# Two linear-attention layers with film conditioning: the film projection with the conditions stationary in four 32-column groups, its matrix moving, and the prologue in another order

## The reference, cut to what matters

```python
xn = layernorm(x)
q = softmax(xn @ Wq + bq, axis=features of a head)
k = softmax(xn @ Wk + bk + mask, axis=tokens)
v = (xn @ Wv + bv) * mask
y = q @ (k.T @ v)                         # per head, 8 heads in layer 0, 16 in layer 1
scale, shift = split(silu(emb) @ W_emb + b_emb)     # (8, 1024): the film projection
h = layernorm(y) * (1 + scale) + shift
x = x + silu(h) @ W_out + b_out
```

## Time and profile before

| | us |
|---|---|
| median of 3 runs (lowest to highest) | 915.04 (914.07 to 915.22) |
| the profiled execution | 913.57 |
| its span | 911.8 |
| PE busy | 865.9 |
| DVE busy | 717.8 |
| ACT busy | 536.2 |
| POOL busy | 382.9 |
| granted clock, mean over the span | 0.966 |

### The profile page before, as it was taken

How to read it: one execution, slowest core, us unless ns; L and a number is a source line. 1 busy time by engine, 2 the same in 40 slices (tenths; PEclk the granted TensorE clock), 3 DMA queues, 4 the chain that set the end, 5 groups by cost and what they waited for, 6 DMA issues and landing times.

```text
span 911.8 us, 14285 instructions
## 1 busy us (share of the span) xinstructions
PE 865.9 (95%) x5405; PEld 494.7 (54%) x5405; DVE 717.8 (79%) x1508; ACT 536.2 (59%) x911; POOL 382.9 (42%) x328
## 2 busy tenths in 40 slices
PE   4689999999999999899999999999999999999967
PEld 4248555475654655445455555555464555555544
DVE  5786987787867879989787878778697878777674
ACT  4256284854748647394765747383856647484713
POOL 1223253443434535453453544553443635455402
PEclk9697999989989999999999999999999999999988
DMA  9824124351643613434232534434442414323222
GB/s 324 334 47 93 59 47 105 90 142 59 185 105 76 156 58 93 104 93 105 48 91 66 111 79 93 105 93 105 71 108 50 108 59 100 98 47 93 47 47 93
DMA packets 168629, 90.86 MB, mean 100 GB/s; under 512 B 134736, under 2 KB 144240, under 8 KB 168560
## 3 DMA queue, kind: packets, MB, share of 16 engines
q1 hardware_dynamic: 168560, 89.94, 39.3%
HBM read 39.60 MB, written 16.78 MB: 62 GB/s over the span
## 4 chain that ended last, share of the span: by engine, by line
PE 73%; DVE 14%; issue 5%; ACT 4%; POOL 2%; DMA 1%; SPq 1%; DVEq 0%
PE ring L411 59%; PE ring L444 6%; PE att_ps L411 4%; PE film_ps L411 3%; DVE sb_w_lo L692 1%; DVE sb_y_stats L931 1%; DVE sb_kt_or_y L927 1%; POOL sb_ht_lo L1176 1%; DVE sb_v_or_q L887 1%; DVE sb_q_max L890 1%; ACT sb_tanh L1053 1%; ACT sb_k_or_qt L1031 1%; ACT sb_kq_hi L1039 1%; ACT sb_xh_or_h L1060 1%; DVE sb_v_or_q L859 1%
## 5 line engine op out<-in xcount | busy, mean ns | idle before, releaser
L411 PE MATMUL ring<-sb_w_hi,sb_xt_hi 128*128 128x512 f16 x512 | 194.8, 380 | 2.3 <-DVE sb_k_max L803 2.2
L411 PE MATMUL ring<-sb_w_lo,sb_xt_hi 128*128 128x512 f16 x512 | 194.8, 380 | 0.0
L411 PE MATMUL ring<-sb_w_hi,sb_xt_lo 128*128 128x512 f16 x512 | 194.6, 380 | 0.0
L1026 ACT ACTIVATE sb_kt_or_y<-sb_kt_or_y,sb_y_add,sb_y_rstd 128x512 f32<-128x512 f32 x64 | 46.9, 804 | 177.9 <-DVE sb_y_add L939 177.9
L1176 POOL TENSOR_TENSOR sb_ht_lo<-sb_xh_or_h,sb_ht_hi 128x512 f16<-128x512 f32 x60 | 68.5, 1174 | 114.5 <-ACT sb_ht_hi L1021 114.5
L411 PE MATMUL ring<-sb_xt_hi,sb_w_hi 128*128 128x512 f16 x256 | 98.1, 383 | 8.6 <-DVE sb_xt_lo L968 8.6
L411 PE MATMUL ring<-sb_xt_lo,sb_w_hi 128*128 128x512 f16 x256 | 98.0, 383 | 0.0
L411 PE MATMUL ring<-sb_xt_hi,sb_w_lo 128*128 128x512 f16 x256 | 98.0, 383 | 0.0
L411 PE MATMUL ring<-sb_w_hi,sb_ht_hi 128*128 128x512 f16 x240 | 92.0, 383 | 1.9 <-ACT sb_xh_or_h L1011 1.5
L411 PE MATMUL ring<-sb_w_lo,sb_ht_hi 128*128 128x512 f16 x240 | 91.8, 382 | 0.0
L411 PE MATMUL ring<-sb_w_hi,sb_ht_lo 128*128 128x512 f16 x240 | 91.3, 380 | 0.0
(11 more groups left out here) (174 smaller groups left out, 1832.2 us busy)
## 6 DMA issues: line engine op xcount, KB each, us to landing
out<-sb_x SPq DMA_DIRECT2D x15, 1024.0 KB, 5.1
sb_x<-out SPq DMA_DIRECT2D x8, 1024.0 KB, 6.1
sb_x<-in_x SPq DMA_DIRECT2D x7, 1024.0 KB, 8.2
sb_mask_raw<-in_mask SPq DMA_DIRECT2D x16, 256.0 KB, 5.8
sb_wemb<-in_L_cond_film_emb_W SPq DMA_DIRECT2D x8, 512.0 KB, 4.9
sb_w_stage<-in_L_cond_Wk SPq DMA_DIRECT2D x2, 1024.0 KB, 6.1
sb_w_hi<-in_L_cond_W_emb SPq DMA_DIRECT2D x1, 1536.0 KB, 15.9
sb_w_lo<-in_L_cond_W_emb SPq DMA_DIRECT2D x1, 1536.0 KB, 17.1
```

The source lines that it names most:

```text
L411: last = nc.tensor.matmul(out, lhs, rhs, start=(n == 0), stop=(n == len(pairs) - 1))
L1026: nc.scalar.activation(kt_or_y[:, t, :], kt_or_y[:, t, :], ACT.Identity, bias=y_add[:, t:t + 1], scale=y_rstd[:, t:t + 1]).then_inc(yh_rea ...
```

## The change

The conditions become the stationary operand, in `emb_wide`, eight blocks of 128x32 of which 24 columns are zero, and 128x512 pieces of `W_emb` the moving one. `film_product(layer, half)` makes 512 of the 1024 outputs with eight f32 matmuls: block k goes to the column group k % 4, so it writes the partitions 32 (k % 4) and up of `film_ps`, and each group sums two of the eight blocks. The result lies with conditions on partitions, in four parts. `copy_film` copies it to `film_rows`, and `turn_film` makes eight f32 matmuls with 128x128 of `film_rows` stationary and a 128x8 selection matrix `pick` moving, which adds the four parts and turns them into the layout that `gather_film` reads.

Layer 0's halves stand in the prologue and behind V tile 1 of step 0, `turn_film(0)` behind XT of step 0. Layer 1's halves stand in steps 6 and 7, `turn_film(1)` behind the first K tile of step 8, and `gather_film(1)`, `bound_film(1)` and `film_tables(1)` move from step 5 to step 8. The loads of layer 1's matrix go from eight of 512 KB in steps 0 to 4 to two pairs of 1024 KB in steps 5 and 7. In the prologue the mask is transposed first, x's transposes run tile by tile, DVE's list is in another order, and POOL's `x_power(1)` stands ahead of `add_bias(0, 0)`.

```diff
-        wemb = sb("wemb", [P, 2, KE, P], F32)
+        wemb = sb("wemb", [P, C, D], F32)
...
-        emb = sb("emb", [P, KE, B], F32)
-        emb_half = sb("emb_half", [P, KE, B], F32)
-        emb_tanh = sb("emb_tanh", [P, KE, B], F32)
+        emb_wide = sb("emb_wide", [P, KE, 32], F32)
+        pick = sb("pick", [P, B], F32)
+        film_rows = sb("film_rows", [P, 2, D], F32)
+
+
+        emb, emb_half, emb_tanh = (film_rows[:, 0, i * KE * B:(i + 1) * KE * B].rearrange("p (k b) -> p k b", k=KE)
+                                   for i in range(3))
...
-            def load_wemb0(begin, end):
-                for half in range(2):
-                    rows = wemb_d[0][half * E // 2:(half + 1) * E // 2, :].rearrange("(k p) n -> p k n", p=P)
-                    sp.dma_start(wemb0[half][:, :, begin:end], rows[:, :, begin:end]).then_inc(wemb0_loaded[begin > 0], 16)
-
-            def load_wemb1(n):
-
-                if n:
-                    sp.wait_ge(film_summed, 2 * C + 2 * n)
-                for j in (2 * n, 2 * n + 1):
-                    sp.dma_start(wemb[:, j % 2], wemb_d[1].rearrange("(k p) n -> p k n", p=P)[:, :, j * P:j * P + P]
-                                 ).then_inc(wemb_loaded[j % 2], 16)
+            def load_wemb0(half):
+                n = slice(half * D, half * D + D)
+                for part in range(2):
+                    rows = wemb_d[0][part * E // 2:(part + 1) * E // 2, :].rearrange("(k p) n -> p k n", p=P)
+                    sp.dma_start(wemb0[part][:, :, n], rows[:, :, n]).then_inc(wemb0_loaded[half], 16)
+
+            def load_wemb1(half):
+
+                sp.wait_ge(w_ready[1], O_ + 1)
+                if half:
+                    sp.wait_ge(film_half, 3)
+                for part, dst in enumerate((wemb, w_stage)):
+                    rows = wemb_d[1][part * E // 2:(part + 1) * E // 2, :].rearrange("(k p) n -> p k n", p=P)
+                    sp.dma_start(dst[:], rows[:, :, half * D:half * D + D]).then_inc(wemb_loaded, 16)
...
-                if 2 <= u <= 4:
-                    load_wemb1(u - 1)
+                if u in (B - 3, B - 1):
+                    load_wemb1(u > B - 3)
...
-            load_wemb0(0, 2 * P)
+            sp.dma_start(mask_rows, mask0_d.rearrange("b (t p) -> (b t) p", p=P)).then_inc(mask_rows_loaded, 16)
+            sp.dma_start(emb, emb_d).then_inc(emb_loaded, 16)
+            load_wemb0(0)
...
-            load_wemb0(2 * P, 2 * D)
+            load_wemb0(1)
...
-            load_wemb1(0)
...
-            def sum_film(layer, js):
-
-                if 0 in js and layer == 0:
+            def film_product(layer, half):
+
+                if layer == 0:
                     pe.wait_ge(emb_ready, 1)
-                for j in js:
-                    if layer == 0:
-                        pe.wait_ge(wemb0_loaded[j > 1], 32)
-                        w = lambda k: wemb0[k // 4][:, k % 4, j * P:j * P + P]
-                    else:
-                        pe.wait_ge(wemb_loaded[j % 2], 16 * (j // 2 + 1))
-                        w = lambda k: wemb[:, j % 2, k, :]
-                    product(film_ps[:, j * B:j * B + B], [(w(k), emb[:, k, :]) for k in range(KE)]).then_inc(film_summed, 1)
+                    pe.wait_ge(wemb0_loaded[half], 32)
+                    w = lambda k: wemb0[k // 4][:, k % 4, half * D:half * D + D]
+                else:
+                    pe.wait_ge(wemb_loaded, 32 * (half + 1))
+                    w = lambda k: (wemb, w_stage)[k // 4][:, k % 4, :]
+                if half:
+                    pe.wait_ge(film_copied, 2 * layer + 1)
+                for k in range(KE):
+                    g = slice(k % 4 * 32, k % 4 * 32 + 32)
+                    last = nc.tensor.matmul(film_ps[g, :], emb_wide[:, k, :], w(k), start=(k < 4), stop=(k >= 4))
+                last.then_inc(film_half, 1)
+
+            def turn_film(layer):
+
+                pe.wait_ge(pick_ready, 1)
+                pe.wait_ge(film_copied, 2 * layer + 2)
+                for j in range(2 * C):
+                    n = j % C * P
+                    last = nc.tensor.matmul(film_ps[:, j * B:j * B + B], film_rows[:, j // C, n:n + P], pick[:], start=True, stop=True)
+                last.then_inc(film_summed, 1)
...
-                    pe.wait_ge(w_scale_ready, 4 + u - 1)
-                    sum_film(1, (2 * u - 2, 2 * u - 1))
                     sum_w(1, u - 1)
-                if u == 5:
+                if u == B - 2:
+                    pe.wait_ge(w_scale_ready, 8)
+                if u in (B - 2, B - 1):
+                    film_product(1, u - B + 2)
+                if u == B:
                     bound_film(1)
...
-                    if u == 0 and i < 2:
-                        sum_film(0, [2 + i])
+                    if u == 0 and i == 1:
+                        film_product(0, 1)
...
+                    if u == B and i == 0:
+                        turn_film(1)
...
-                    sum_film(0, range(4, 2 * C))
+                    turn_film(0)
...
+            pe.wait_ge(ident_loaded, 16)
+            pe.wait_ge(mask_rows_loaded, 16)
+            nc.tensor.transpose(att_ps[:, 0, 0:B * T], mask_rows, ident[0:B * T, 0:B * T]).then_inc(mask_turned, 1)
+            pe.wait_ge(mask_cols_ready, 1)
             sum_ln()
-            pe.wait_ge(ident_loaded, 16)
-            turn_x(-1)
-            pe.wait_ge(mask_rows_loaded, 16)
+            banks = [take_bank("XT", c, -1) for c in range(C)]
+            for t in range(T):
+                pe.wait_ge(xh_ready, t + 1)
+                for c in range(C):
+                    turned = nc.tensor.transpose(banks[c][:, t * P:t * P + P], xh_or_h[:, t, c * P:c * P + P], ident[:])
+                    if t == T - 1:
+                        turned.then_inc(done["XT"], 1)
             pe.wait_ge(ln_ready, 2)
-            nc.tensor.transpose(att_ps[:, 0, 0:B * T], mask_rows[:], ident[0:B * T, 0:B * T]).then_inc(mask_turned, 1)
-            pe.wait_ge(mask_cols_ready, 1)
             sum_w(0, K_)
-            sum_film(0, (0, 1))
+            film_product(0, 0)
...
+            def copy_film(layer, half):
+
+                dve.wait_ge(film_half, 2 * layer + half + 1)
+                nc.vector.tensor_copy(film_rows[:, half, :], film_ps[:]).then_inc(film_copied, 1)
...
-                dve.wait_ge(film_summed, 2 * C * (layer + 1))
+                dve.wait_ge(film_summed, layer + 1)
...
+                    quarters = ident[:].rearrange("p (g r) -> p r g", g=4)
+                    nc.vector.tensor_reduce(pick[:], quarters[:, 0:B, :], AX_X, ALU.add).then_inc(pick_ready, 1)
...
-                    elif u == 5:
+                    elif u == B:
...
-                    elif u == 5:
+                    elif u == B:
                         film_tables(1)
                         output_scale(1)
+                    elif u in (B - 2, B - 1):
+                        copy_film(1, u - B + 2)
...
-            dve.wait_ge(cols_loaded, 16)
-            for layer in range(LAYERS):
-                ln_peaks(layer)
+            link(nc.vector.memset(emb_wide[:], 0.0))
...
-            ln_scales(0)
-            x_affine(0)
-
-            dve.wait_ge(emb_loaded, 16)
-            link(nc.vector.tensor_scalar(emb_half[:], emb[:], 0.5, None, ALU.mult))
-            dve.wait_ge(emb_tanh_ready, 1)
-            nc.vector.scalar_tensor_tensor(out=emb[:], in0=emb_tanh[:], scalar=1.0, in1=emb_half[:], op0=ALU.add, op1=ALU.mult
-                                           ).then_inc(emb_ready, 1)
-            find_peak(0, K_)
             dve.wait_ge(mask_turned, 1)
             nc.vector.tensor_copy(mask_cols[:], att_ps[:, 0, 0:B * T]).then_inc(mask_cols_ready, 1)
+            dve.wait_ge(cols_loaded, 16)
+            ln_peaks(0)
+            x_affine(0)
+            ln_peaks(1)
+            dve.wait_ge(emb_loaded, 16)
+            link(nc.vector.tensor_scalar(emb_half, emb, 0.5, None, ALU.mult))
+            ln_scales(0)
+            find_peak(0, K_)
+            dve.wait_ge(emb_tanh_ready, 1)
+            nc.vector.scalar_tensor_tensor(out=emb_wide[:, :, 0:B], in0=emb_tanh, scalar=1.0, in1=emb_half, op0=ALU.add, op1=ALU.mult
+                                           ).then_inc(emb_ready, 1)
...
+            def copy_film(half):
+
+                act.wait_ge(film_half, half + 1)
+                nc.scalar.copy(film_rows[:, half, :], film_ps[:]).then_inc(film_copied, 1)
...
+                if u == 0:
+                    copy_film(1)
...
+            copy_film(0)
...
+            x_power(1)
             pool.wait_ge(row_bias_loaded[0], 48)
             add_bias(0, 0)
-            x_power(1)
```

11 lines of the change are left out of this document (5 added, 6 removed).

## The result

The change makes the kernel 1.6% faster: 899.62 us median of 4 runs (897.69 to 900.33) against 914.87 (914.07 to 915.22), a ratio of 0.9837, 95% interval 0.9822 to 0.9852. The profiled execution took 897.69 us, its span 895.9; that is 15.9 us less than the 911.8 of before.

What follows compares the result with a forecast made beforehand. PE bounds the kernel at 50.30 us a step, with a second chain through DVE, ACT and POOL close behind. Terms: 20.3 + 4.4 - 6.8 - 5.9 = 12.0 us gained, forecast median 903.0 us, range 897 to 911.

Steps and rivals of the forecast that it cites:

- steps 1 to 5: Steps without film products: 279.26 us falls to 259.0, DVE's chain keeping 7.5 us of surplus; gain 20.3 us.
- halves, steps 6 and 7: One half of layer 1's product on PE in each step, both 54.2 us; cost 2.9 + 3.9 = 6.8 us.
- step 8 with the turn: `turn_film(1)` on PE, 1.8 us, plus the 4.15 us that step 5 loses with `gather_film` and tables; cost 5.9 us.
- step 0: `attend` starts 2.9 us earlier, `gather_film(0)` leaves DVE's path (0.6), V's last tile comes earlier (0.9); gain 4.4 us.
- a: Time of one half, eight float32 products in four column groups on PE: 3.9 us, sixteen records in nine slots of 0.44.
- serial end: Eight products of a half one after the other, no overlap: 7.0 us a half, 909 us in all; chance 0.2.
- parallel end: Four products of a half side by side in their column groups: 1.8 us a half.
- records keep their order, so only the second record of one product and the first of the next can overlap: Claim about PE's records in a half: sixteen take nine slots of 0.44 us, hence 3.9 us.
- groups side by side: Rival for the halves: column groups run in parallel, 1.8 us a half, 4.2 us less in steps 6 and 7; chance 0.2.
- the rival that speaks of loads: Peak searches wait for weights loaded no earlier; steps 2 to 5 lose 1.5 us more each, 909 us; chance 0.12.
- the prologue gains and loses the same: POOL's bias moved behind `x_power(1)`: K starts some 3 us earlier, DVE's low halves in step 0 lose 1.0 us each.
- the slower case: Rival: new 32-column products leave the clock at 1.2 GHz, a serial half takes 14.0 us, 923 us; chance 0.05.

Runs made afterwards that it cites:

- neighbours share: Changed kernel with products 0 and 1 of a half in column group 0, 2 and 3 in group 1 and so on; 898.44 us, ratio 0.9831.
- bias late: Kernel before the change, with POOL computing `x_power(1)` ahead of the bias addition of unit 0; 914.87 us, ratio 1.0005.
- gather early: Changed kernel with `gather_film(1)` moved within step 8 from ahead of the first Q row to behind the reciprocal of k's sums; 894.61 us, ratio 0.9781.
- the five others with the same step 0: Five variants of the changed kernel that leave its step 0 as it is; their profiles have `k_shift(1)` at 107.39 to 107.75 us.
- bias first: Changed kernel with POOL adding the bias of unit 0 ahead of `x_power(1)` again; 893.88 us, ratio 0.9797.

## Why the prediction was right, and where it was wrong

Each part as the forecast put it, against the profiles:

| part | forecast | measured | from |
|---|---|---|---|
| steps 1 to 5 | gain 20.3 | 19.4 | 279.26 - (364.88 - 104.98 = 259.90) |
| halves, steps 6 and 7 | cost 6.8 | 2.8 | (52.30 - 51.33) + (54.00 - 50.30 - 1.85) |
| step 8 with the turn | cost 5.9 | 6.1 | (54.53 - 50.30) + 1.85 |
| step 0 | gain 4.4 | 5.3 | 110.32 - 104.98 |
| sum | gain 12.0 | 15.8 | spans: 15.9 |

**The mis-sized term** is a, the half of a product: 3.9 us forecast, 1.85 measured. The serial end (7.0) and the parallel end (1.8) were both right to 0.05 us; the choice between them was wrong. The step that failed is "records keep their order, so only the second record of one product and the first of the next can overlap": neighbours share shows records of later products starting first. The rival "groups side by side", chance 0.2, said 899, and 899.6 came. The sum missed by 3.8 us, this row by 4.0; the misses of the other rows, -0.9, -0.2 and +0.9, cancel but for 0.2. The time lies in the range because the range was drawn to reach this rival.

**Steps 1 to 5** held, that the DVE chain keeps most of steps 2 to 4 above all: 53.24, 52.00 and 52.80 for 53.8, 52.1 and 52.5. This was the larger decision: PE's busy time fell by 28.5 us, and the kernel gained 15.9. But the forecast explained the surplus by searches and low halves, and the rival that speaks of loads expected them to be late only afterwards. The waits of 1.90, 1.67 and 2.07 us were in the measured offsets all along, and grew by 0.2 to 0.7 us where the rival had 1.5. The gain hangs on the profile of before as well: against the one with the bias late, whose steps 1 to 5 add up to 280.9 us, it is 21.0. Step 1 is 51.47, not 50.3. Its offset is 17.40, near step 7's, but PE waits 0.95 us for POOL's low part of v, as it did before the change (0.96), which the forecast left out, and 0.89 ahead of `attend`, which the film products had covered; no run tells what it would take to remove these.

**Step 8** held to 0.2 us, by carrying over the 4.15 of step 5; the gather early shows that 2.7 of it belonged to the place and not to the work.

**Step 0** came out near the forecast in the change's own profile, and that is partly luck: in the five others with the same step 0 the gain is 2.6 to 2.9 us against the same 110.32, where 4.4 was forecast. `attend` waits 5.37 us for q's second transposing load, until 84.79, where the forecast had 87.2 before DVE's gains; in those five it starts at 87.3 to 87.6, behind the stretch at 1.2 GHz. That PE waits there and the products that stood in front were partly free is as forecast. The line "the prologue gains and loses the same" is true of the kernel before, as bias late shows, and wrong of the changed one, where the bias would not have delayed K in its old place; some 2.4 us were left there. The forecast read the price from a trace in which the bias landed 0.4 us behind the start of DVE's low halves of Wk; with the change's prologue it lands 2.5 us behind it.

**Not seen:** the clock in layer 1's new products stays at 1.00, so the slower case had no ground there; the second pair of loads brought no wait.

## What to carry to other kernels

A product with few columns on the stationary side costs by what moves, and here groups that write different partitions divided that time by their number, the two records of float32 included: weigh such a change from its serial end divided by the groups. When work leaves the bounding engine, list the second chain step by step, and split each of its stretches into work and waits for data: here what looked like the price of a search was a wait for the one shared buffer and a search behind it, and taking the wait away saved 5.5 us and left the work whole, more than leaving out three quarters of the search (4.2). Before an operation is moved, read again in the new order what it will stand beside; a good part of its price belonged to its neighbour, not to itself.

## What the runs showed of the hardware

Float32 matmuls of 512 columns leave two records of 0.436 us each; in four 32-column groups sixteen of them end after 1.85 us, in two after 3.56, in one after 6.98. Records in different groups start out of program order: in neighbours share two of products 4 to 7 start at 392.09, with six of the eight records of products 0 to 3 still to come, from 392.52 on.

Behind sixteen float32 products with 8 moving columns the 16 transposes take 3.65, 3.65 and 3.58 us in steps 2 to 4 of the kernel before, at a granted clock of 0.50 to 0.57, and 1.94 in step 1; behind two such products they take 1.94 or 1.95 in every step, at 1.00.

Beside POOL's operations on 128x512, a DVE operation on 128x32 takes 1.08 us instead of 0.19, and the low halves of k 1.57 to 1.70 us instead of 0.75 each, while the peak search (2.28 us) keeps its pace. Beside a power of 128x4 on POOL the first three operations on 128x32 keep theirs (gather early). With bias first, four of `xt_lo` take 2.49 us as without POOL, and it is POOL's addition that takes 3.78 us instead of 1.26; in the two other profiles with the bias first it takes 3.55 and 4.09. The Trainium skill, SBUF — State Buffer, in its section on SBUF's two sides, says that the two engines share one pair of ports as an exclusive lock, taken by a DVE operation in a mode that uses both ports or with two SBUF inputs, the latter only against a POOL operation that reads SBUF, and that whoever comes first keeps it for the whole instruction. The rows agree for the low halves, and for the search, which has one input. L762 has a single input and was slowed all the same, 0.96 for 0.18 us; that would be the page's first case, but no row here names the mode. For the addition they go further than the page: it starts at 24.79 beside the last of Wk's low halves and gets through only behind four more DVE operations, the `xt_lo` that end at 27.45, not behind one.
